# First edge aggregation of a two-layer graph network: both degrees from one 16-bit product per tile, one-hots made tile by tile

## The reference, cut to what matters

```python
deg = jnp.maximum(jax.ops.segment_sum(jnp.ones(dst.shape, jnp.float32), dst, num_segments=6250), 1.0)
deg_isqrt = deg ** (-0.5)                        # scales rows in layer 0
xn = _layernorm(x, axis=-1)
msgs = edge_vals[:, None] * xn[edge_src]          # layer 0, edge_vals = edge_weight
agg = jax.ops.segment_sum(msgs, edge_dst, num_segments=N)
...
deg = jax.ops.segment_sum(ew, dst, num_segments=n_nodes) + 1.0   # layer 1, weighted degree
dinv = jnp.where(deg > 0, jax.lax.rsqrt(deg), 0.0)
```

## Time and profile before

| what | us |
|---|---|
| median of three runs | 4429.74 (4424.64 to 4432.52) |
| profiled execution: span from its first to its last instruction | 3913.9 |
| first aggregation (first gather issued 121.99, last 1161.84) | about 1043 of the span |
| second aggregation (`d.t1`) | about 988 |
| third aggregation (`d.t2`) | about 997 |

### The profile page before, as it was taken

How to read it: one execution, slowest core, us unless ns; L and a number is a source line. 1 busy time by engine, 2 the same in 40 slices (tenths; PEclk the granted TensorE clock), 3 DMA queues, 4 the chain that set the end, 5 groups by cost and what they waited for, 6 DMA issues and landing times. The chain is left out here.

```text
span 3913.9 us, 41587 instructions
## 1 busy us (share of the span) xinstructions
PE 2817.2 (72%) x12730; PEld 2139.6 (55%) x12730; DVE 1759.8 (45%) x4424; ACT 768.9 (20%) x1634; POOL 2555.5 (65%) x2689
## 2 busy tenths in 40 slices
PE   3577877777768647667777777665677777777778
PEld 2466656656544535556555555544466555556557
DVE  6433335555524842443333333332355555555533
ACT  1111101111103313321111111110122222222210
POOL 3677777777760342557777777775777777777701
PEclk9999988888879879889989999887889999999969
DMA  4344434444433457754444444433344444444405
GB/s 139 116 117 120 124 107 139 130 138 131 129 96 94 143 164 202 213 179 133 138 117 125 124 125 125 114 111 97 109 123 122 124 124 123 123 121 125 125 21 197
DMA packets 279533, 501.68 MB, mean 128 GB/s; under 512 B 59771, under 2 KB 179969, under 8 KB 279162
## 3 DMA queue, kind: packets, MB, share of 16 engines
q0 software_dynamic: 126240, 345.85, 30.9%
q1 hardware_dynamic: 135916, 139.10, 11.5%
q10 hardware_dynamic: 17136, 13.84, 1.1%
HBM read 419.12 MB, written 79.18 MB: 127 GB/s over the span
## 5 line engine op out<-in xcount | busy, mean ns | idle before, releaser
L1476 PE MATMUL bank<-g,m 128*128 128x256 f32 (+1 forms) x4704 | 1466.0, 436 | 806.4 <-DMA g<-d_t,src_i 537.4
L1399 POOL DMA_INDIRECT g<-d_t,src_i x1568 | 1505.2, 960 | 511.4 <-issue 511.4
L1476 PEld LDWEIGHTS bank<-g,m 128*128 128x128 f32 x4704 | 879.6, 211 | 1102.3 <-issue 400.1
L1399 POOL DMA_INDIRECT g<-d_xn,src_i x784 | 802.3, 1023 | 244.3 <-issue 242.5
L1424 DVE TENSOR_SCALAR m<-iota,rel_f,ew_f 128x128 f32<-128x128 f32 x1568 | 421.6, 365 | 255.9 <-PE bank L1476 250.4
L1440 DVE TENSOR_TENSOR accT<-bank,accT 128x256 f32 x294 | 122.8, 418 | 593.1 <-PE bank L1464 592.9
L1405 ACT ACTIVATE s<-bank 128x256 f32<-128x256 f32 (+1 forms) x294 | 111.4, 379 | 1076.0 <-PE bank L1478 554.7
L1427 DVE TENSOR_TENSOR eq<-iota,rel_f 128x1024 bf16<-128x1024 f32 x98 | 119.9, 1224 | 138.3 <-PE bank L1478 138.3
L1478 PE MATMUL bank<-ones_b,eq 128*128 128x1 bf16 x784 | 136.9, 175 | 0.0
L1340 PE MATMUL bank<-wg,side_lg 128*128 128x256 f32 (+1 forms) x392 | 132.1, 428 | 2.9 <-DVE side_lg L1332 2.9
L219 POOL TENSOR_TENSOR rsd<-ved,mhalf 128x2 f32<-128x2 f32 (+1 forms) x25 | 19.0, 760 | 175.6 <-DVE ved L213 175.4
(11 more groups left out here) (387 smaller groups left out, 4273.3 us busy)
## 6 DMA issues: line engine op xcount, KB each, us to landing
g<-d_t,src_i POOLq DMA_INDIRECT x1568, 2.8
side_xn<-d_xn SPq DMA_DIRECT2D x96, 256.0 KB, 3.1
g<-d_xn,src_i POOLq DMA_INDIRECT x784, 2.8
d_swT<-wkv SPq DMA_DIRECT2D x48, 256.0 KB, 3.0
swT<-d_swT SPq DMA_DIRECT2D x24, 512.0 KB, 3.8
xt<-d_xs POOLq DMA_DIRECT2D x80, 128.0 KB, 3.0
d_ys<-y ACTq DMA_DIRECT2D x80, 128.0 KB, 2.6
x<-in_x SPq DMA_DIRECT2D x24, 256.0 KB, 2.7
```

The lines of the kernel that those rows point to most:

```text
L1399: pool.indirect_dma_start(g[n % RING][:, u, 0:D], None, table, bass.IndirectOffsetOnAxis(ap=k.src_i[:, t:t + 1], axis=0)).then_inc(gathere ...
L1476: ins = pe.matmul(b[:, 0:GW], m[o][:, u, :], g[r][:, u, :], start=(u == 0), stop=(u == GT - 1 and not count))
```

## The change

`stage_aggregate`, with `count` only: the gathered rows are 256 wide, without the column of ones. Once per two groups DVE splits the 16 columns of weights into three 16-bit parts that add up to the fp32 weight exactly, beside a constant 1, in `ew_b` (`split`). `prepare` then makes `eq` and `m` tile by tile, sixteen instructions per group. PE multiplies `ew_b` (four columns, as the weights it loads) with `eq` (128 columns, moving) into rows 0 to 3 of columns 256 to 383 of the window's own bank; both degrees so come out already turned, and the turn of the degree columns goes. `finish` adds four rows to `dinv` from that bank; so a group's first tile now also waits for the addition two groups back (`acc_added`) and for the split. `stage_gnn_first` moves four rows in place of two and adds the three parts.

```diff
-    GW = D + 1 if count else D
-    SW = GW + 1 if count else D
-        g = [st.sb(f"g{r}", [P, GT, GW]) for r in range(RING)]
+        g = [st.sb(f"g{r}", [P, GT, D]) for r in range(RING)]
+        ew_b = [st.sb(f"ew_b{j}", [P, SPLIT * GT, 4], BF16) for j in range(2)] if count else []
...
+            def split(j):
+                ew = k.ew_f[:, j * SPLIT * GT:min((j + 1) * SPLIT, NG) * GT]
+                parts = ew_b[j % 2][:, 0:ew.shape[1], :]
+                left = rest[:, 0:ew.shape[1]]
+                dve.memset(parts[:, :, 1], 1.0)
+                dve.tensor_copy(parts[:, :, 0], ew).then_inc(split_done, 1)
+                wait(dve, split_done, 4 * j + 1)
+                dve.tensor_tensor(left, ew, parts[:, :, 0], ALU.subtract).then_inc(split_done, 1)
+                wait(dve, split_done, 4 * j + 2)
+                dve.tensor_copy(parts[:, :, 2], left).then_inc(split_done, 1)
+                wait(dve, split_done, 4 * j + 3)
+                dve.tensor_tensor(parts[:, :, 3], left, parts[:, :, 2], ALU.subtract).then_inc(split_done, 1)
...
-                dve.tensor_tensor(eq[r][:], k.iota[:].rearrange("p (a n) -> p a n", a=1).to_broadcast([P, GT, P]),
-                                  k.rel_f[:, e].rearrange("p (u a) -> p u a", a=1).to_broadcast([P, GT, P]), ALU.is_equal).then_inc(eq_done, 1)
-                wait(dve, eq_done, n + 1)
-                dve.tensor_tensor(m[r][:], eq[r][:], k.ew_f[:, e].rearrange("p (u a) -> p u a", a=1).to_broadcast([P, GT, P]), ALU.mult).then_inc(m_done, 1)
+                if count and n % SPLIT == 0:
+                    split(n // SPLIT)
+                for u in range(GT):
+                    t = n * GT + u
+                    if count:
+                        dve.tensor_scalar(eq[r][:, u, :], k.iota[:], k.rel_f[:, t:t + 1], None, ALU.is_equal)
+                    ins = dve.tensor_scalar(m[r][:, u, :], k.iota[:], k.rel_f[:, t:t + 1], k.ew_f[:, t:t + 1], ALU.is_equal, ALU.mult)
+                ins.then_inc(m_done, 1)
...
-                    to = k.dinv[0:2, bass.ds(base, WIN)]
-                    dve.tensor_tensor(to, k.bank[7][0:2, D:D + WIN], to, ALU.add)
+                    to = k.dinv[0:4, bass.ds(base, WIN)]
+                    dve.tensor_tensor(to, k.bank[n % 2][0:4, D:D + WIN], to, ALU.add)
...
-                if count:
-                    pe.transpose(k.bank[7][0:2, D:D + WIN], s[n % 2][:, D:SW], k.ident[:])
...
+                        wait(pe, acc_added, n - 1)
+                        wait(pe, split_done, 4 * (n // SPLIT + 1))
...
-                ins = pe.matmul(b[:, 0:GW], m[o][:, u, :], g[r][:, u, :], start=(u == 0), stop=(u == GT - 1 and not count))
-                if count:
-                    ins = pe.matmul(b[:, GW:SW], eq[o][:, u, :], k.ones_b[:, 0:1], start=False, stop=(u == GT - 1))
+                def degrees():
+                    t = n % SPLIT * GT + u
+                    pe.matmul(b[0:4, D:D + WIN], ew_b[n // SPLIT % 2][:, t, :], eq[o][:, u, :], start=False, stop=False)
+                if count and u > 0:
+                    degrees()
+                ins = pe.matmul(b[:, 0:D], m[o][:, u, :], g[r][:, u, :], start=(u == 0), stop=(u == GT - 1))
+                if count and u == 0:
+                    degrees()
...
-                sp.dma_start(d.deg, k.dinv[0:2, 0:NTILE * P]).then_inc(deg_moved, 16)
+                sp.dma_start(d.deg, k.dinv[0:4, 0:NTILE * P]).then_inc(deg_moved, 16)
...
                         wait(dve, deg_moved, 32)
+                        dve.tensor_tensor(degt[:, 2, :], degt[:, 2, :], degt[:, 3, :], ALU.add).then_inc(joined, 1)
+                        wait(dve, joined, 1)
+                        dve.tensor_tensor(degt[:, 0, :], degt[:, 0, :], degt[:, 2, :], ALU.add).then_inc(joined, 1)
                         dve.tensor_scalar(degt[:, 1, :], degt[:, 1, :], 1.0, None, ALU.max).then_inc(raised, 1)
+                        wait(dve, joined, 2)
```

More of the change, by code:

```diff
@@ L1362, in stage_aggregate @@
     k = kit
-    RING, ONEHOTS = 4, 3
-    GW = D + 1 if count else D
-    SW = GW + 1 if count else D
+    RING, ONEHOTS, SPLIT = 4, 3, 2
     with Stage(nc, kit) as st:
         side = side_of(st, a, d)
-        g = [st.sb(f"g{r}", [P, GT, GW]) for r in range(RING)]
+        g = [st.sb(f"g{r}", [P, GT, D]) for r in range(RING)]
         m = [st.sb(f"m{r}", [P, GT, P]) for r in range(ONEHOTS)]
         eq = [st.sb(f"eq{r}", [P, GT, P], BF16) for r in range(ONEHOTS)] if count else []
-        s = [st.sb(f"s{h}", [P, SW]) for h in range(2)]
+        ew_b = [st.sb(f"ew_b{j}", [P, SPLIT * GT, 4], BF16) for j in range(2)] if count else []
+        rest = st.sb("rest", [P, SPLIT * GT]) if count else None
+        s = [st.sb(f"s{h}", [P, D]) for h in range(2)]
         drow = st.sb("drow", [P, P], I32)
@@ L1375, in stage_aggregate @@
         gathered = [[st.pool_dma(f"gathered{r}_{h}") for h in range(2)] for r in range(RING)]
-        eq_done, m_done, multiplied, copied, window_turned, acc_added, ones_set = (
-            st.sem(n) for n in ("eq_done", "m_done", "multiplied", "copied", "window_turned", "acc_added", "ones_set"))
+        m_done, multiplied, copied, window_turned, acc_added, split_done = (
+            st.sem(n) for n in ("m_done", "multiplied", "copied", "window_turned", "acc_added", "split_done"))
         blank, cleared, row_loaded, dup_done, idx_done, weighted, row_done, scattered, at_loaded, at_turned = (
@@ L1418, in prepare @@
                 r = n % ONEHOTS
-                e = slice(n * GT, (n + 1) * GT)
                 wait(dve, multiplied, n - ONEHOTS + 1)
-                if not count:
-                    for u in range(GT):
-                        t = n * GT + u
-                        ins = dve.tensor_scalar(m[r][:, u, :], k.iota[:], k.rel_f[:, t:t + 1], k.ew_f[:, t:t + 1], ALU.is_equal, ALU.mult)
-                    ins.then_inc(m_done, 1)
-                    return
-                dve.tensor_tensor(eq[r][:], k.iota[:].rearrange("p (a n) -> p a n", a=1).to_broadcast([P, GT, P]),
-                                  k.rel_f[:, e].rearrange("p (u a) -> p u a", a=1).to_broadcast([P, GT, P]), ALU.is_equal).then_inc(eq_done, 1)
-                wait(dve, eq_done, n + 1)
-                dve.tensor_tensor(m[r][:], eq[r][:], k.ew_f[:, e].rearrange("p (u a) -> p u a", a=1).to_broadcast([P, GT, P]), ALU.mult).then_inc(m_done, 1)
+                if count and n % SPLIT == 0:
[6 more added lines that the diff above has]
+                ins.then_inc(m_done, 1)
             def finish(n):
@@ L1436, in finish @@
                 if count:
-                    to = k.dinv[0:2, bass.ds(base, WIN)]
-                    dve.tensor_tensor(to, k.bank[7][0:2, D:D + WIN], to, ALU.add)
+                    to = k.dinv[0:4, bass.ds(base, WIN)]
+                    dve.tensor_tensor(to, k.bank[n % 2][0:4, D:D + WIN], to, ALU.add)
                 at = k.accT[:, :, bass.ds(base, WIN)]
                 dve.tensor_tensor(at, chunks(k.bank[7]), at, ALU.add).then_inc(acc_added, 1)
-            if count:
-                for r in range(RING):
-                    ins = dve.memset(g[r][:, :, D:D + 1], 1.0)
-                ins.then_inc(ones_set, 1)
             prepare(0)
@@ L1472, in tile @@
                     if count:
-                        wait(pe, ones_set, 1)
+                        wait(pe, acc_added, n - 1)
+                        wait(pe, split_done, 4 * (n // SPLIT + 1))
                 if u % 4 == 0:
                     wait(pe, gathered[r][u // 4], 64 * (n // RING + 1))
-                ins = pe.matmul(b[:, 0:GW], m[o][:, u, :], g[r][:, u, :], start=(u == 0), stop=(u == GT - 1 and not count))
-                if count:
-                    ins = pe.matmul(b[:, GW:SW], eq[o][:, u, :], k.ones_b[:, 0:1], start=False, stop=(u == GT - 1))
+                def degrees():
[6 more added lines that the diff above has]
+                    degrees()
                 if u == GT - 1:
@@ L1696, in stage_gnn_first @@
         wxT = [st.sb(f"wxT{j}", [SDIM, D]) for j in range(2)]
[L1697 removed]
+        degt = st.sb("degt", [NTILE, 4, P])
         pos = st.sb("posd", [NTILE, P])
         z_done, kept, stat_done = (st.sem(s) for s in ("z_done", "kept", "stat_done"))
[L1700 removed]
+        deg_moved, joined, raised, rooted, wd_psum = (st.sem(s) for s in ("deg_moved", "joined", "raised", "rooted", "wd_psum"))
         wfirst, wld = st.sem("wfirst"), st.sem("wld")
@@ L1830, in _ @@
                         wait(dve, rooted, 1)
-                        dve.reciprocal(degt[:], degt[:]).then_inc(raised, 1)
+                        dve.reciprocal(degt[:, 0:2, :], degt[:, 0:2, :]).then_inc(raised, 1)
                         wait(dve, raised, 5)
```

12 lines of the change are left out of this document (5 added, 7 removed).

## The result

The change made the kernel slower. Its median is 4460.87 us (4437.78 to 4477.64, eight executions) against 4423.86 for the kernel before beside it (4406.79 to 4432.52, eight); the ratio is 1.0079, with a 95% interval of 1.0056 to 1.0102. The prediction was 4388, with a range of 4372 to 4408. The profiled execution of after took 4445.24 us with a span of 4443.7: only 1.5 us lie outside the span. In the profile of before it had been 515.8.

The account below looks back on a forecast made before the run. The prediction took POOL's gathers to bound the first aggregation: 802.3 - 46.3 + 5 = 761 us, a stage shorter by 41, span 3873 for 3913.9. With 515.8 us outside unchanged, the median goes from 4429.7 to 4388, range 4372 to 4408.

Parts of the forecast that it names:

- The bound: First aggregation: POOL never waits, PE follows it, so the stage is as long as 784 gathers with their gaps, 1040.8 us.
- the 515.8 us outside the span: Whole kernel: time outside the profiled span of 3913.9 us, taken as unchanged to get from span to median.
- a sign against me: Whole kernel: a span 41 us shorter with a median that isn't would show the forecast wrong.
- The gathers: First aggregation: dropping whole-group one-hots frees 46.3 us, new rows cost 5 (0 to 10); POOL busy 761 us.
- holds in the side work: First aggregation: gathers held by side instructions with two SBUF operands, 13.4 us; after the change anywhere from 0 to 37.
- rival 2: First aggregation: rows of one-hots hold gathers to the row's end, 353 us less 46, about 4737; 3 in 100.
- The rule of the Trainium skill: One-hots: VectorE's `tensor_scalar` can take the port pair shared with GpSimd, making 1568 blocking instructions; the forecast went against it.
- 0 to 784 x 0.113 = 89 us, hidden behind 239 us of waiting: First aggregation, PE: added price of the degree product over the old count's product; 137 us of waiting left, path cost nothing.
- DVE, the split, the degrees behind the stage: DVE: 4.8 us more per two-group round, split 1.1 of it, covered by 9.1 idle; degrees behind: nothing, or 0.6 us.
- Rivals 1 and 3: One-hots: 16-bit ones hold gathers, 22 us back, 4410, 5 in 100; DVE becomes the bound, about 4490, 4 in 100.
- Rival 4: POOL freed, time not returned: side holds worsen (24 us), something outside the span grows (19 us); about 4428; 5 in 100.

Follow-up runs that it names:

- no_degrees: The kernel after without its 784 degree products (both degrees left out of the result), all else kept: 0.9957 of before (0.9930 to 0.9983), first aggregation 1127 us.
- the two second profiles: The kernel before, unchanged, profiled once more: ratio 0.9999, span 4354.2 us; and the kernel after, unchanged, measured again: 1.0051 of before.

## Why the prediction was wrong, point by point

**The bound.** "POOL runs freely from the first gather to the last" was true of the execution that was read, and not of the other one of this kernel that was profiled. The step that failed first is the one that took "the 515.8 us outside the span" as they are. It was a difference of a profiled span and a timed median, and no row showed anything outside. In the second profile of before 1.6 us lie outside (4355.77 - 4354.2), and 415 of the 440 us are in the aggregations, with POOL waiting. I had named a median that doesn't follow the span as a sign against me; the sign was already there, before the change.

**The gathers.** What holds a gather, and that one-hots with one SBUF operand don't, came out nearly as said: POOL's busy time went from 802.3 to 773.2 where 761 was forecast, the mean gather from 1.023 to 0.986. Of 275 gathers that begin inside a one-hot after the change 228 take at most 1.0 us, and together the 275 lose 15.5 us where 5 were put, with 0 to 10 as bounds; holds in the side work cost about as much as before (13.4). Four of the 275 lose 2.0 to 2.4 us each, 9 of the 15.5, and end within 0.9 us of the end of their row of one-hots, as rival 2 has it for all; this is one of them:

```profile
537.50 3.30 POOL L1399 DMA_INDIRECT g<-d_xn,src_i  x1 [0.30 <-issue]
...
539.65 0.33 DVE L1439 TENSOR_SCALAR m<-iota,rel_f,ew_f 128x128 f32<-128x128 f32 x1
...
541.10 0.95 POOL L1399 DMA_INDIRECT g<-d_xn,src_i  x1 [0.30 <-issue]
```

What sets these four apart is not shown. The rule of the Trainium skill that had the blocking the other way round ("SBUF — State Buffer", section "Who interferes with whom") is not borne out by the other 271 gathers. But the 29 us were no gain, since POOL waits for PE anyway.

**PE.** "0 to 784 x 0.113 = 89 us, hidden behind 239 us of waiting" is the second step that failed. The product itself took 227 ns, between the 175 and 288 of the bounds. What was left out is what stands ahead of its load: 0.33 us of pause per tile, 188 us net per stage in the tile's distance. The bound was taken from the durations of products, and a duration doesn't hold the time in front. The trace of before had a hint, two weight loads of the first aggregation, in columns as in the earlier trace rows:

```profile
L1478 PEld LDWEIGHTS bank<-ones_b,eq 128*128 128x128 bf16 x784 | 84.1, 107 | 30.6
L1462 PEld LDWEIGHTS bank<-ident,s 128*2 128x2 f32 x98 | 9.0, 92 | 15.4 <-issue 5.5 <-ACT s L1405 0.8
```

The load of 128 columns has 0.04 us of idle time ahead of it, the load of 2 columns has 0.16. The price of a narrow load stood in the idle column of a row whose busy time I used. And the cover, PE's 239 us of waiting for gathers, is 15.6 us in the second profile of before, and no more than 52.1 if all of PE's idle time ahead of the message products is counted.

**The sizes.** Of the 0.5 to 0.8% the degrees alone give 0.36% (0.12 to 0.59) and the one-hots alone 0.16%, which is not told from nothing. The 188 us on PE lengthened the stage by only 12 us between the two second profiles (1149 against 1137, medians of before 4372 and 4374 in their groups), and the late results shrank from 411 to 224 us. That the one made room for the other is read from these sums; no run of its own shows it.

**DVE, the split, the degrees behind the stage.** DVE's busy time rose to 642.8 us in the stage and it stayed off the path: in no_degrees, with all of DVE's new work, the time is under before. Rivals 1 and 3 did not come (of 113 gathers that begin inside a 16-bit one-hot 111 take at most 1.0 us), and of rival 2 only the four gathers above. Rival 4, freed gathers whose time doesn't come back, is what happened to that half of the change, for another reason than the one named. That PE becomes the bound was not among the rivals; it was ruled out by waiting that only one execution had.

## What to carry to other kernels

Lay the profiled span beside the timed runs before reading anything else: where they differ by more than a few us, the profile may be of another execution than the one that counts, and every wait in it, above all "this engine never waits", needs a second profile. Price an added operation from the start of its neighbour to the start of the next, with the idle column of its load, and not from its duration. A small matrix as the loaded operand is no small product: padding it to the full 128 columns, with junk, took the whole loss away, though that only brings the kernel back to where it was; no version here that makes both degrees beats the kernel before.

## What the runs showed of the hardware that I had not expected

A weight load of 4 or 32 columns behind a product on 128 loaded columns waits mostly 0.33 us at the full clock, 0.65 at half of it and 0.17 where the product ahead moves 128 columns and not 256; one of 128 columns mostly 0.03 or less, and inside a row of narrow ones only the first waits. TensorE's results can reach the other engines long after the end of their rows: in the second profile of before 55 of 98 were over 1 us late, half of these over 7.5 and one 19.9. That came with 16 gathers in a round of 23 us and was gone with 8, but one execution with 16 was free of it too. The granted clock was no measure of the time: a first aggregation took 1189 us from its first gather to its last at 0.92, 1137 at 0.82 and 1140 at 0.73.
